# Attention: softmax sums and totals moved by DMAs on Pool's queue, with reciprocals four steps later and LayerNorm's scaling on Pool

## The chip, the cores and the metric

One core of one Trainium2 chip runs the whole program. The metric is the device time of one execution in microseconds, median of several runs. Engines are named as in the profile: PE (TensorE), with its weight loads as PEld, DVE (VectorE), ACT (ScalarE), POOL (GpSimd) and SP (SyncE, which here only issues DMAs).

## The reference

Input x is 8 batches of 1024 tokens of width 256. The program computes a feed-forward stage with routing, attention, and the feed-forward stage again, each on a LayerNorm of its input and added to it:

```
x = x + 0.5 * ffn(layernorm(x))
x = x + attention(layernorm(x))
x = x + 0.5 * ffn(layernorm(x))

attention:  xd = (x @ W_down).reshape(b, t, 16 heads, 16)
            keys, queries = xd through 16x16 maps per head, each * 16 ** -0.25; values likewise, unscaled
            out = softmax(queries @ keys^T, over keys) @ values        # per batch and head
            return out.reshape(b, t, 256) @ W_unify + b_unify
```

All of it is float32 in and out. Only attention is changed.

## The kernel before

`attention` works through 8 batches; a batch through 4 units g of four heads; a unit through 16 steps t. Steps 0 to 7 hold the first 512 queries (half 0), steps 8 to 15 the others (half 1), and within a half each step takes one block of 128 keys. In step t TensorE does three things:

- `for_exp` (L1360): four score tiles (128 keys x 512 queries, one a head) of step t + 1, into the three banks `pd`. ScalarE's exponentials (L1457) read them and free the banks.
- `for_max` (L1349): scores of step t + 13 with queries on the partitions, in two parts, for VectorE's row maxima (L1521). The maxima travel through a DRAM tensor into extra rows of the query operand, so that the exponential needs no subtraction.
- `times_v` (L1369): four heads' values times the exponentials of step t, summed in one bank `po` over the eight steps of a half. The value operand `va` has 32 columns a head: 16 values, one column of ones, 15 of zeros. So row 16 of a head's 32 rows in `po` holds the softmax totals.

Besides, a step may hold one side tile, placed by the table `side_at` (L1139): xT (transpose of the LayerNorm), xd (W_down), qk, v, all for the next batch, and for the output f, aT and u. A side tile takes a bank of the same ring of three, between the second and the third score tile.

The way of the sums is this. After steps 7 and 15 VectorE copies `po` to `os` (`values_out`, L1547). In the second step of the following half (t = 9, or t = 1 of the next unit) tile f transposes `os` on TensorE (L1378), VectorE takes the reciprocal of the totals (L1578) and multiplies (L1581) into `ao`. Once four units have passed, two tiles aT a half transpose `ao` back (L1378), ScalarE copies them to `aT` (L1478), and two tiles u multiply with W_unify (L1408); VectorE adds x and the bias and SyncE stores. aT and u of half 0 stand in steps 10, 11, 13, 14 of unit 3, those of half 1 in steps 2, 3, 5, 6 of the next batch's unit 0.

LayerNorm of the next batch runs in unit 0: VectorE's statistics in steps 0, 1, 4, 5 (L147 to L160), Pool's power -1/2 in steps 1 and 5 (L165), VectorE's scaling in steps 2, 3, 6, 7 (L173). Pool also splits the keys in two parts (`key_parts`, L1663, L1665) and adds the bias to the residual (L1690, step 8 of unit 2).

Each engine runs one instruction stream, written out by the class `Walk`, which calls each engine's `step` in the same order; nothing is reordered at run time, and a wait holds up everything behind it on its engine. Semaphores order the engines. SyncE's queue carries the loads of heads, maxima, rows and the stores.

Of the kernel before, what the change touches and what calls it, by code (L numbers as in the profile page):

```python
# [21 lines left out]
P = 128  # L22
D = 256
# [1044 lines left out]
def attention(nc, k, w, x_in, x_out, NBAT):  # L1068
# [10 lines left out]

    mscr = nc.dram_tensor("at_mscr", (4, 2, MROWS, 2, NT, P // MB, MB), F32).ap()  # L1080

    x_t, o_t = split_token_tiles(x_in), split_token_tiles(x_out)
    with ExitStack() as ctx:
# [17 lines left out]
        rec = sb("rec", [P, 4, GH], F32)  # L1101
        ao = sb("ao", [P, NT, D], F32)
        aT = sb("aT", [P, DT, NQ], F32)
# [6 lines left out]
        diagonals = Diagonals(ctx, nc, w, k, pb[0], ao[:, :, :])  # L1110

        S = lambda n: Sem(ctx, nc, "at_" + n)
        s_one = ctx.enter_context(nc.semaphore("at_s_one"))
# [6 lines left out]
        s_ld = [[S(f"s_ld{g}{p}") for p in range(2)] for g in range(4)]  # L1120
        s_mr = [S(f"s_mr{g}") for g in range(4)]
# [6 lines left out]
        s_rc = S("s_rc")  # L1128
        s_xl = S("s_xl")
# [7 lines left out]
        OUT = lambda f: [("aT", f, 0), ("aT", f, 1), ("u", f, 0), ("u", f, 1)]  # L1137
# [21 lines left out]
        splits = lambda task: task[0] == "qk"  # L1159
        half = lambda b, g, qh: 2 * unit(b, g) + qh  # L1160
        unit = lambda b, g: 4 * b + g
        next_unit = lambda b, g: (b, g + 1) if g < 3 else (b + 1, 0)

        half_ahead = lambda b, g, t: (b, g, 1) if t < NT else (*next_unit(b, g), 0)
# [10 lines left out]
        class Walk:  # L1175
# [3 lines left out]
            def __init__(self, eng, do):  # L1179
# [15 lines left out]
                do.end([self.place(task, NBAT - 1, 1, 3) for task in [("f", 1)] + OUT(1)])  # L1195
# [8 lines left out]
            def phase(self, do, b, par, g, prev=True, last=False):  # L1204
                for t in range(ST):
# [13 lines left out]
                    elif task == ("f", 1):  # L1219
                        a = self.place(task, *((b, par, g - 1) if g > 0 else (b - 1, 1 - par, 3)))  # L1220
                    elif task and task[0] in ("aT", "u") and g == 0:
# [6 lines left out]

        block = ctx.enter_context(nc.Block())

        @block.sync
        def _(eng):
            for s in (*s_xr, *(x for two in s_ld for x in two), *s_mr, s_ms, s_xl, *s_st):
                s.open(eng)
# [7 lines left out]
            def load_head(ring, b, g, j, parts_in):  # L1242
# [9 lines left out]
                for s, part in enumerate(Q_SLOTS):  # L1252
                    r1 = HALF * e + HS * s
                    src = parts[r0:r0 + HS, 0, part, c, :].rearrange("r (a q) -> r a q", a=2)
                    eng.dma_start(qa[g][r1:r1 + HS, :, p, :].bitcast(F32), src.bitcast(F32)).then_inc(s_ld[g][p].sem, 16)
                for s, part in enumerate(K_SLOTS):
                    r1 = HALF * e + HS * s
                    eng.dma_start(ka[g][r1:r1 + HS, p, :].bitcast(F32),
                                  parts[r0:r0 + HS, 1, part, c, :].bitcast(F32)).then_inc(s_ld[g][p].sem, 16)
# [9 lines left out]
            def load_maxima(b, g, qh):  # L1269
# [7 lines left out]
                for e in range(2):  # L1277
# [3 lines left out]
                    eng.dma_start(to.bitcast(F32), src).then_inc(s_mr[g].sem, 16)  # L1281
# [7 lines left out]
            class Do:  # L1289
# [38 lines left out]
                def end(self, sides):  # L1328
                    for a in sides[3:]:
# [7 lines left out]
        def _(eng):  # L1337
# [3 lines left out]
            def for_max(b, g, t, kh):  # L1341

                qh, p, qt = t // NT, t % NT // 4, t % 4
                if t in (0, NT // 2) and kh == 0:
                    eng.wait_ge(s_ld[g][p].sem, s_ld[g][p].at(16 * ULOADS * (b + 1)))
# [7 lines left out]
            def for_exp(ring, b, g, t, j, n):  # L1353

                qh, kt, e, p = t // NT, t % NT, j % 2, j // 2
                if kt == 0 and j == 0:
                    eng.wait_ge(s_mr[g].sem, s_mr[g].at(16 * MLOADS * (2 * b + qh + 1)))
# [15 lines left out]
            def side_product(ring, a):  # L1373
# [23 lines left out]
                elif a.kind == "f":  # L1397
                    eng.wait_ge(s_o.sem, s_o.at(2 * unit(a.b, a.g) + a.at[0] + 1))
                    mm = turn(lambda j: os_[:, j * P:(j + 1) * P])
                elif a.kind == "aT":  # L1400
                    f, c = a.at
                    mm = turn(lambda j: ao[:, 4 * f + j, c * P:(c + 1) * P])
                else:
                    f, h = a.at
                    for i in range(2):
                        q = (2 * h + i) * P
                        for c in range(DT):
                            mm = eng.matmul(bank[:, i * D:(i + 1) * D], aT[:, c, q:q + P], w.wu[:, c, :],  # L1408
# [3 lines left out]
            class Do:  # L1412
                def before(self, sides):
# [5 lines left out]
                    eng.wait_ge(s_one, 2)  # L1419
# [31 lines left out]
        def _(eng):  # L1451
            for s in (s_hi, *s_free):
# [5 lines left out]

            def side_out(ring, a):
                if a.kind in ("f", "u"):  # L1460
# [3 lines left out]
                if a.kind == "qk":  # L1464
                    c, f = a.at
                    if f == 0:
                        for two in s_ld[2 * c:2 * c + 2]:
                            for s in two:
                                eng.wait_ge(s.sem, s.at(16 * ULOADS * a.b))
# [7 lines left out]
                elif a.kind == "aT":  # L1477
                    ins = eng.activation(aT[:, a.at[1], :], bank[:, :], ACT.Copy)  # L1478
# [6 lines left out]
            class Do:  # L1485
                def before(self, sides):
                    for a in sides:
                        if a.kind == "v":
                            eng.wait_ge(s_one, 2)
# [9 lines left out]
                def step(self, b, par, g, t, coming, tiles, done, a, side, ahead, last):  # L1499
# [4 lines left out]
                    for j in range(2, GH if tiles else 2):  # L1504
                        exponentials(self.ring, t + 1, j, tiles[j])

# [7 lines left out]
        def _(eng):  # L1514
            norm.open_vector(eng)
            for s in (s_xn, s_mx, s_nm, s_o, s_rc):
# [32 lines left out]
            ALL, FIRST, SECOND = range(4), (0, 1), (2, 3)  # L1549

# [185 lines left out]
```

## Time and profile before

| | |
|---|---|
| median of 3 runs | 2889.71 us (2889.34 to 2901.28) |
| the profiled execution | 2896.95 us, span 2895.2 us |
| attention, in the span | about 640 to 2262 us |
| busy in the span | PE 93%, DVE 74%, ACT 63%, POOL 21% |
| granted TensorE clock, mean | 0.964 of full speed |

The busy shares are of the whole span and mix three stages. Matmuls are pipelined, so that a PE shown busy is not necessarily at its peak; idle time of an engine that nobody waits for costs nothing. A row's line number is that of the helper that issues the instruction.

### The profile page before, as it was taken

To read this page: it belongs to the slowest core of one execution; us is meant where nothing else is said; L and a number is where in the kernel's file an instruction comes from. 1 tells how busy PE (TensorE), PEld (TensorE's weight loads), DVE (VectorE), ACT (ScalarE), POOL (GpSimd) and SP (SyncE) were. 2 spreads that over 40 slices of the span, in tenths; PEclk is the share of its full clock that TensorE was granted. 3 is DMA by queue.
4 is the path that set the end of the run, shared out by engine and by line. 5 is a ranking of instruction groups with operands and counts; after the bars stand their busy time and mean duration, and the time that the engine had idled before them with its cause. 6 is when DMAs were issued, how large, how long until landed. Compare 5 with 4: busy or idle time off the path is not lost. (4 is left out here: it accounts for less than half of the span.)

```text
span 2895.2 us, 48611 instructions
## 1 busy us (share of the span) xinstructions
PE 2705.7 (93%) x17009; PEld 1644.3 (57%) x17009; DVE 2145.9 (74%) x3552; ACT 1821.3 (63%) x3409; POOL 599.8 (21%) x562
## 2 busy tenths in 40 slices
PE   5899999867999999999999999999999589999997
PEld 3799999863334334333343343433433368999886
DVE  6555456747899898998998988989895665554574
ACT  5344556632777776777777767777777444444564
POOL 3355114521100100101001001010000235521353
PEclk9899999986999999999999999999999789999998
DMA  5211113414123132131231321312310512111341
GB/s 172 66 44 44 58 45 106 133 60 75 30 50 75 33 61 54 39 62 36 50 75 33 60 55 39 62 37 50 60 28 5 173 30 80 44 44 45 102 133 63
DMA packets 164529, 181.69 MB, mean 63 GB/s; under 512 B 38472, under 2 KB 133904, under 8 KB 164368
## 3 DMA queue, kind: packets, MB, share of 16 engines
q1 hardware_dynamic: 156176, 169.03, 24.0%
q0 software_dynamic: 8192, 10.57, 1.2%
q8 instruction: 94, 1.54, 0.2%
q14 instruction: 67, 0.55, 0.1%
HBM read 97.51 MB, written 31.54 MB: 45 GB/s over the span
## 5 line engine op out<-in xcount | busy, mean ns | idle before, releaser
L1457 ACT ACTIVATE at_ex<-at_pd 128x512 f32<-128x512 f32 x2048 | 1084.7, 600 | 383.7 <-PE at_pd L1360 379.2
L1521 DVE TENSOR_REDUCE at_mxc<-at_pb 128x2 f32<-128x1024 f32 x1024 | 1219.0, 1219 | 120.8 <-PE at_pb L1349 113.8
L768 DVE TENSOR_TENSOR f_ml_hl<-f_ml_h,f_ml_hh 128x512 fp32r<-128x512 f32 (+1 forms) x384 | 287.8, 751 | 422.7 <-ACT f_ml_hh L844 421.5
L1360 PE MATMUL at_pd<-at_qa,at_ka 50*128 50x512 f32 x2048 | 583.6, 469 | 3.9 <-ACT at_ex L1457 3.2
L1360 PEld LDWEIGHTS at_pd<-at_qa,at_ka 50*128 50x128 f32 x2048 | 266.6, 185 | 538.4 <-issue 349.2
L1369 PE MATMUL at_po<-at_ex,at_va 128*32 128x512 f32 x4096 | 548.8, 608 | 0.2 <-ACT at_ex L1457 0.2
L841 ACT ACTIVATE f_ml_h<-f_ml_pL,b1T 128x512 f32<-128x512 f32 (+1 forms) x384 | 243.8, 635 | 457.9 <-PE f_ml_pL L895 446.3
L1349 PE MATMUL at_pb<-at_ka,at_qa 48*128 48x512 f32 x2048 | 433.1, 450 | 24.7 <-DVE at_mxc L1521 16.5
L910 PE MATMUL f_ml_pA<-f_wh,f_ml_hh 128*128 128x256 f32 (+1 forms) x1408 | 410.4, 291 | 3.7 <-DVE f_ml_hl L768 3.7
L912 PE MATMUL f_ml_pA<-f_wl,f_ml_hh 128*128 128x256 f32 (+1 forms) x1408 | 402.5, 286 | 0.0
L913 PE MATMUL f_ml_pA<-f_wh,f_ml_hl 128*128 128x256 f32 (+1 forms) x1408 | 402.5, 286 | 0.0
L1349 PEld LDWEIGHTS at_pb<-at_ka,at_qa 48*128 48x128 f32 x2048 | 196.0, 188 | 191.0 <-DVE at_mxc L1521 129.0
L893 PE MATMUL f_ml_pL<-f_ml_xTh,f_wh 128*128 128x512 f32 (+1 forms) x768 | 286.5, 373 | 2.8 <-DVE f_ml_xTl L763 2.8
L894 PE MATMUL f_ml_pL<-f_ml_xTl,f_wh 128*128 128x512 f32 (+1 forms) x768 | 286.2, 373 | 0.0
L895 PE MATMUL f_ml_pL<-f_ml_xTh,f_wl 128*128 128x512 f32 (+1 forms) x768 | 283.0, 368 | 0.0
L910 PEld LDWEIGHTS f_ml_pA<-f_wh,f_ml_hh 128*128 128x128 f32 (+1 forms) x1408 | 265.9, 189 | 15.9 <-DVE f_ml_hl L768 5.2
L912 PEld LDWEIGHTS f_ml_pA<-f_wl,f_ml_hh 128*128 128x128 f32 (+1 forms) x1408 | 266.0, 189 | 7.1
L913 PEld LDWEIGHTS f_ml_pA<-f_wh,f_ml_hl 128*128 128x128 f32 (+1 forms) x1408 | 265.7, 189 | 0.0
L844 ACT ACTIVATE f_ml_hh<-f_ml_h 128x512 fp32r<-128x512 f32 (+1 forms) x384 | 222.2, 579 | 20.0
L165 POOL TENSOR_TENSOR f_ml_ln_rstd<-f_ml_ln_ve,neghalf 128x4 f32<-128x4 f32 (+1 forms) x48 | 52.8, 1101 | 562.5 <-DVE f_ml_ln_ve L160 562.5
L165 POOL TENSOR_TENSOR at_ln_rstd<-at_ln_ve,neghalf 128x4 f32<-128x4 f32 x16 | 16.2, 1014 | 714.8 <-DVE at_ln_ve L160 714.8
L895 PEld LDWEIGHTS f_ml_pL<-f_ml_xTh,f_wl 128*128 128x128 f32 x768 | 148.0, 193 | 22.5
(128 smaller groups left out, 2636.6 us busy)
## 6 DMA issues: line engine op xcount, KB each, us to landing
f_wraw<-in_L_ffn_w SPq DMA_DIRECT2D x128, 256.0 KB, 2.8
at_qa<-at_parts SPq DMA_DIRECT2D x384, 64.0 KB, 2.4
at_ka<-at_parts SPq DMA_DIRECT2D x384, 64.0 KB, 2.4
f_ro_xr<-in_L_attn_x SPq DMA_DIRECT2D x16, 512.0 KB, 3.9
f_ml_xr<-in_L_attn_x SPq DMA_DIRECT2D x16, 512.0 KB, 4.2
x<-f_ml_yo SPq DMA_DIRECT2D x16, 512.0 KB, 4.0
at_xr<-x SPq DMA_DIRECT2D x16, 512.0 KB, 5.1
at_xres<-x SPq DMA_DIRECT2D x8, 1024.0 KB
```

The lines of the kernel that those rows point to most:

```text
L768: eng.tensor_tensor(hl[h % RING][:, 0:w], h32[h % 2][:, 0:w], hh[h % RING][:, 0:w].bitcast(F32), ALU.subtract).then_inc(s_lo.sem, 1)
L893: eng.matmul(out, W1(wh[wb], c, h), xTh[b][:, c, 0:w], start=(c == 0), stop=False)
L894: eng.matmul(out, W1(wh[wb], c, h), xTl[b][:, c, 0:w], start=False, stop=False)
L895: mm = eng.matmul(out, W1(wl[wb], c, h), xTh[b][:, c, 0:w], start=False, stop=(c == DT - 1))
L910: eng.matmul(out, hi, W2(wh[wb], h), start=(h == 0 and j % 2 == 0), stop=False, skip_group_check=True)
L912: eng.matmul(out, hi, W2(wl[wb], h), start=False, stop=False, skip_group_check=True)
L913: mm = eng.matmul(out, lo, W2(wh[wb], h), start=False, stop=(h == HT - 1), skip_group_check=True)
L1349: mm = eng.matmul(pb[kh][:, e * NQ:(e + 1) * NQ], qa[g][rows, qh, p, qt * P:(qt + 1) * P], ka[g][rows, p, kh * NQ:(kh + 1) * NQ], start=Tr ...
L1360: eng.matmul(pd[n % RING][:, :], ka[g][rows, p, kt * P:(kt + 1) * P], qa[g][rows, qh, p, :], start=True, stop=True).then_inc(s_full.sem, 1)
L1369: mm = eng.matmul(po[VW * j:VW * (j + 1), :], va[par][:, kt, GH * g + j, :], ex[t % 2][:, j, :], start=(kt == 0), stop=(kt == NT - 1), ski ...
L1457: eng.activation(ex[t % 2][:, j, :], pd[n % RING][:, :], ACT.Exp).then_inc(s_free[n % RING].sem, 1)
L1521: eng.tensor_reduce(mxc[:, t // NT, kh, t % NT::NT], pb[kh][:, :].rearrange("p (e k) -> p e k", e=2), AX.X, ALU.max, negate=True).then_inc ...
```

## The change

- The tiles f and aT are gone, with the tensors `ao` and `rec`. The side table places u of both halves in unit 0 of the next batch (steps 2, 4, 10, 11), and the tiles xT, xd are moved by some steps.
- ScalarE copies `po` to `os`, at the end of steps 7 and 15, behind that step's exponentials.
- Pool issues five DMAs a half. They write the sums to DRAM (`sums_out`, one step after the copy's), read the totals into `tot` (128 x 16) and the values into `aT` (`sums_in`), write the reciprocals (`totals_out`) and read them, each row 16 times, into `den` (`totals_in`). Each stage waits for the landing of the one before. `divide` multiplies `aT` with `den` on Pool once two units' heads fill 128 partitions.
- VectorE takes the reciprocals of `tot` in steps 4 and 12.
- Pool takes the power and the scaling of LayerNorm (`normalize`, steps 5 and 12 of unit 0). VectorE's statistics are in steps 2, 4, 10, 11.
- The columns 16 to 31 of a head in `va` are all ones. The load semaphores of heads are merged, so that a unit other than 0 waits for all its heads at once. Pool's bias is in step 14.

```diff
-            table = {1: ("f", 1), 9: ("f", 0)}
-            if g == 0 and not prev:
-                del table[1]
+            table = {}
             if g == 0 and prev:
-                table.update(zip((2, 3, 5, 6), OUT(1)))
-            if g == 3:
-                table.update(zip((10, 11, 13, 14), OUT(0)))
+                table.update(zip((2, 4, 10, 11), OUT(0) + OUT(1)))
+            if g == 3 and last:
+                table.update(zip((14, 15), OUT(0)))
             if g == 0 and not last:
-                table.update(zip((7, 8, 10, 11, 13, 14), XT + XD))
+                table.update(zip((7, 8, 12, 13, 14), [*XT[:2], XD[0], *XT[2:]]))
             if g == 1 and not last:
-                table.update(zip((2, 3, 5, 6, 7, 8), XD[-2:] + QK))
+                table.update(zip((1, 2, 3, 5, 6, 7, 8), XD[1:] + QK))
...
+            def values_out(b, g, t):
+                eng.wait_ge(s_pv.sem, s_pv.at(ST * unit(b, g) + t + 1))
+                if half(b, g, t // NT):
+                    eng.wait_ge(s_os.sem, s_os.at(16 * half(b, g, t // NT)))
+                eng.activation(os_[:, :], po[:, :], ACT.Copy).then_inc(s_o.sem, 1)
...
-            def values_out(b, g, t):
-                eng.wait_ge(s_pv.sem, s_pv.at(ST * unit(b, g) + t + 1))
-                eng.tensor_copy(os_[:, :], po[:, :]).then_inc(s_o.sem, 1)
+            def reciprocals(b, g, qh):
+                eng.wait_ge(s_td.sem, s_td.at(16 * (half(b, g, qh) + 1)))
+                eng.reciprocal(tot[:, :], tot[:, :]).then_inc(s_rc.sem, 1)
...
+            def normalize(ring, b, f, read):
+
+                norm.pow_step(eng, 2 * b + f, 4)
+                if read is not None:
+                    eng.wait_ge(s_full.sem, s_full.at(ring.full(read)))
+                at = slice(4 * f, 4 * f + 4)
+                norm.apply_step(eng, 2 * b + f, xn[:, at, :], xr[:, at, :], [P] * 4).then_inc(s_xn.sem, 1)
+
+            def sums_out(b, g, qh):
+                eng.wait_ge(s_o.sem, s_o.at(half(b, g, qh) + 1))
+                eng.dma_start(oscr[g, qh, :, :, :].rearrange("j r q -> (j r) q"), os_[:, :]).then_inc(s_os.sem, 16)
+
+            def sums_in(ring, b, g, qh, read):
+                eng.wait_ge(s_os.sem, s_os.at(16 * (half(b, g, qh) + 1)))
+                eng.dma_start(tot[:, :], oscr[g, qh, :, HS, :].rearrange("j (x y) -> j x y", y=HS)).then_inc(s_td.sem, 16)
+                if b > 0:
+                    eng.wait_ge(s_full.sem, s_full.at(ring.full(read)))
+                r0 = HS * GH * (g % 2)
+                eng.dma_start(aT[r0:r0 + HS * GH, qh, g // 2, :], oscr[g, qh, :, 0:HS, :]).then_inc(s_nd.sem, 16)
+
+            def totals_out(b, g, qh):
+                eng.wait_ge(s_rc.sem, s_rc.at(2 + half(b, g, qh) + 1))
+                eng.dma_start(rscr[g, qh, :, :].rearrange("j (x y) -> (j x) y", y=HS), tot[:, :]).then_inc(s_rs.sem, 16)
+
+            def totals_in(b, g, qh):
+                eng.wait_ge(s_rs.sem, s_rs.at(16 * (half(b, g, qh) + 1)))
+                if b > 0 or g > 1:
+                    eng.wait_ge(s_dv.sem, s_dv.at(4 * b + 2 * (g // 2) + qh - 1))
+                r0 = HS * GH * (g % 2)
+                src = rscr[g, qh, :, :].unsqueeze(1).broadcast_to([GH, HS, NQ])
+                eng.dma_start(den[r0:r0 + HS * GH, qh, :], src).then_inc(s_nd.sem, 16)
+
+            def divide(b, g, qh):
+                eng.wait_ge(s_nd.sem, s_nd.at(16 * 2 * (half(b, g, qh) + 1)))
+                if g % 2:
+                    eng.tensor_tensor(aT[:, qh, g // 2, :], aT[:, qh, g // 2, :], den[:, qh, :],
+                                      ALU.mult).then_inc(s_dv.sem, 1)
...
+                    past = (b, g, 0) if t >= NT else (*before(b, g), 1) if b or g else None
+                    if past and t % NT == 0:
+                        sums_out(*past)
+                    if past and t % NT == 1:
+                        sums_in(self.ring, *past, self.read[past[2]])
+                    if past and t % NT == 5:
+                        totals_out(*past)
+                    if past and t % NT == 6:
+                        totals_in(*past)
+                    if g == 0 and not last and t in (5, 12):
+                        normalize(self.ring, b + 1, t // 8, side)
+                    if past and t % NT == 7:
+                        divide(*past)
```

TensorE's tile u waits for `divide` of its half (`s_dv`). At the end Pool runs the five transfers and `divide` once more for the last half.

## Rows read from the trace of the kernel before

**Rows 1.** Windows, amid attention: PE, PEld, DVE, ACT, POOL busy us, clock, DMA share, GB/s.
```profile
1000.00:1100.00 100.00, 100.00 (x624) 40.11 (x620) 91.27 (x104) 76.29 (x151) 5.00 (x4) 1.00 0.34 66
```

**Rows 2.** Timeline: plain step 0 of batch 1; start us, length us, engine, line, operation.
```profile
899.96 1.06 PE L1369 MATMUL at_po<-at_ex,at_va 128*32 128x512 f32 x8
900.96 0.50 PE L1360 MATMUL at_pd<-at_qa,at_ka 50*128 50x512 f32 x2
901.40 0.68 DVE L1547 COPY at_os<-at_po 128x512 f32<-128x512 f32 x1
901.49 2.06 ACT L1457 ACTIVATE at_ex<-at_pd 128x512 f32<-128x512 f32 x4 [0.54 <-PE at_pd L1360]
902.14 0.18 PEld L1360 LDWEIGHTS at_pd<-at_qa,at_ka 50*128 50x128 f32 x1 [0.30 <-ACT at_ex L1457]
902.57 1.06 PE L1369 MATMUL at_po<-at_ex,at_va 128*32 128x512 f32 x8
```

**Rows 3.** Timeline: batch 1, group 0, from step 1 to xT's tile of step 7.
```profile
905.66 1.07 PE L1369 MATMUL at_po<-at_ex,at_va 128*32 128x512 f32 x8
...
912.14 1.06 PE L1369 MATMUL at_po<-at_ex,at_va 128*32 128x512 f32 x8
...
915.55 1.07 PE L1369 MATMUL at_po<-at_ex,at_va 128*32 128x512 f32 x8
...
919.80 1.06 PE L1369 MATMUL at_po<-at_ex,at_va 128*32 128x512 f32 x8
...
922.45 0.17 DVE L160 TENSOR_SCALAR at_ln_ve<-at_ln_mv 128x4 f32<-128x4 f32 x1
...
924.04 1.06 PE L1369 MATMUL at_po<-at_ex,at_va 128*32 128x512 f32 x8
...
925.70 0.66 PE L1378 MATMUL at_pd<-ident,at_xn 128*128 128x128 f32 x4
```

**Rows 4.** Timeline: batch 1, group 3, from step 9 to step 10.
```profile
1074.11 1.06 PE L1369 MATMUL at_po<-at_ex,at_va 128*32 128x512 f32 x8
...
1077.20 1.06 PE L1369 MATMUL at_po<-at_ex,at_va 128*32 128x512 f32 x8
```

**Rows 5.** Groups of instructions by line: count, busy us, mean ns, idle time before.
```profile
L700 POOL DMA_INDIRECT out<-f_ml_yo,f_ml_idx x24 | 24.3, 1012 | 20.2 <-DVE f_ml_yo L789 13.8 <-issue 6.4
...
L1663 POOL CAST at_parts<-at_xn 128x512 fp32r<-128x512 f32 x32 | 19.5, 609 | 271.2 <-ACT at_xn L1482 271.2
...
L1478 ACT ACTIVATE at_aT<-at_pd 128x512 f32<-128x512 f32 x32 | 19.3, 604 | 6.1 <-PE at_pd L1378 5.8
...
L165 POOL TENSOR_TENSOR at_ln_rstd<-at_ln_ve,neghalf 128x4 f32<-128x4 f32 x16 | 16.2, 1014 | 714.8 <-DVE at_ln_ve L160 714.8
```

**Rows 6.** The tile at_xres: Pool's operations on it, ns min/median/max.
```profile
L1690 POOL TENSOR_TENSOR at_xres<-at_xres,at_bu x32: 1265/1282/1308, 809.2 to 2157.1; 128x512 f32<-128x512 f32 x32
```

**Rows 7.** DMA issues: queue, count, KB each, median us from issue to landing.
```profile
at_xr<-x SPq DMA_DIRECT2D x16, 512.0 KB, 5.1
...
x<-at_yo SPq DMA_DIRECT2D x32, 256.0 KB, 2.2
...
f_ml_xr<-x,f_ml_idx POOLq DMA_INDIRECT x24, 3.5
```

**Rows 8.** Timeline: last unit, the V products of step 7.
```profile
2217.83 1.93 PE L1369 MATMUL at_po<-at_ex,at_va 128*32 128x512 f32 x8
```

**Rows 9.** Windows: last unit, the granted clock.
```profile
2220.00:2225.00 5.00, 4.74 (x17) 1.48 (x16) 0.53 (x1) 2.48 (x5) 0.00 (x0) 0.50 0.00 0
```

**Rows 10.** Timeline: attention's end and the next stage's first load.
```profile
2244.79 1.06 PE L1369 MATMUL at_po<-at_ex,at_va 128*32 128x512 f32 x8 [0.18 <-ACT at_ex L1457]
2245.92 0.69 DVE L1547 COPY at_os<-at_po 128x512 f32<-128x512 f32 x1 [2.01 <-PE at_po L1369]
...
2251.89 3.63 PE L1408 MATMUL at_pd<-at_wu,at_aT 128*128 128x256 f32 x8 [0.78 <-ACT at_aT L1478]
...
2262.06 2.03 SPq L259 DMA_DIRECT2D f_ro_xr<-x  x4
```

More of the change, by code:

```diff
@@ L1119, in attention @@
         s_kp = S("s_kp")
-        s_ld = [[S(f"s_ld{g}{p}") for p in range(2)] for g in range(4)]
-        s_mr = [S(f"s_mr{g}") for g in range(4)]
+        s_ld = [S("s_ld"), *[S(f"s_ld{g}") for g in range(4)]]
+        s_mr = [S(f"s_mr{i}") for i in range(2)]
         s_b = S("s_b")
@@ L1162, in attention @@
         next_unit = lambda b, g: (b, g + 1) if g < 3 else (b + 1, 0)
+        before = lambda b, g: (b, g - 1) if g else (b - 1, 3)
         half_ahead = lambda b, g, t: (b, g, 1) if t < NT else (*next_unit(b, g), 0)
@@ L1194, in __init__ @@
                         self.phase(do, b, b % 2, g, prev=b > 0, last=b == NBAT - 1)
-                do.end([self.place(task, NBAT - 1, 1, 3) for task in [("f", 1)] + OUT(1)])
+                do.end([self.place(task, NBAT - 1, 1, 3) for task in OUT(1)])
             def place(self, task, b, par, g):
@@ L1227, in phase, with units_landed @@
                     do.step(b, par, g, t, coming, tiles, done, a, side, ahead, last)
+        def units_landed(eng, b, c):
+            for g, p in ((0, 0), (0, 1), (1, 0)) if c == 0 else ((2, 0), (3, 0)):
+                eng.wait_ge(landed(g, p).sem, landed(g, p).at(loads(g, b)))
         block = ctx.enter_context(nc.Block())
@@ L1232, in _ @@
         def _(eng):
-            for s in (*s_xr, *(x for two in s_ld for x in two), *s_mr, s_ms, s_xl, *s_st):
+            for s in (*s_xr, *s_ld, *s_mr, s_ms, s_xl, *s_st):
                 s.open(eng)
@@ L1258, in load_head @@
                     eng.dma_start(ka[g][r1:r1 + HS, p, :].bitcast(F32),
-                                  parts[r0:r0 + HS, 1, part, c, :].bitcast(F32)).then_inc(s_ld[g][p].sem, 16)
+                                  parts[r0:r0 + HS, 1, part, c, :].bitcast(F32)).then_inc(landed(g, p).sem, 16)
             def ones():
@@ L1328, in end @@
                 def end(self, sides):
-                    for a in sides[3:]:
+                    for a in sides:
                         store_out(self.ring, a)
@@ L1451, in _ @@
         def _(eng):
-            for s in (s_hi, *s_free):
+            for s in (s_hi, s_o, *s_free):
                 s.open(eng)
@@ L1631, in step @@
                         turn(*half_ahead(b, g, t))
-                    if t % NT == NT - 1:
-                        values_out(b, g, t)
-                    if g == 0 and not last and t < 8:
-                        f, q = t // 4, t % 4
-                        if q < 2:
-                            stats(b + 1, f, (FIRST, SECOND)[q])
-                        else:
-                            apply(self.ring, b + 1, f, side, (FIRST, SECOND)[q - 2])
+                    if t == NT + 4:
+                        reciprocals(b, g, 0)
+                    if t == 4 and (b or g):
+                        reciprocals(*before(b, g), 1)
+                    if g == 0 and not last and t in STATS_AT:
+                        stats(b + 1, *STATS_AT[t])
                 def end(self, sides):
+                    reciprocals(NBAT - 1, 3, 1)
                     for a in sides:
@@ L1694, in end @@
                 def end(self, sides):
-                    pass
+                    past = (NBAT - 1, 3, 1)
+                    sums_out(*past)
+                    sums_in(self.ring, *past, self.read[1])
+                    totals_out(*past)
+                    totals_in(*past)
+                    divide(*past)
             Walk(eng, Do())
```

100 lines of the change are left out of this document (43 added, 57 removed).

## The prediction

> **What bounds the kernel now.** I read the page first: of the span's 2895 us, attention holds 640 to 2262 and the change touches nothing else, so everything below is about those 1620 us. The table of windows comes next. In a stretch in the middle of attention TensorE is busy all the time at a granted clock of 1.00 (its 2.4 GHz level), VectorE for 91% and ScalarE for 76% [rows 1]. A TensorE busy for 100% in modelled records does not yet say which engine sets the pace, so I went to the timeline of one step.
>
> There are 512 steps (8 batches x 4 head groups x 16), and each ends with one group of eight products with V on L1369. The distance between the starts of two such groups is the length of a step. A step with nothing on the side takes 2.61 us (899.96 to 902.57, [rows 2]). Inside it a loop closes: the first score product starts at 900.96, ScalarE has no work for 0.54 us until it lands, its exponential begins at 901.49, and the fourth score product (loading at 902.14, idle 0.30 on ScalarE) needs the bank which that exponential frees, because there are three banks for four tiles. Then come the products with V, then the next step. So a plain step is bound by this loop through TensorE and ScalarE. VectorE's two maxima (2.35 us together) fit beside it. Even the step in which VectorE also copies the sums (0.68 us at 901.40) is 2.61 long: that copy costs nothing today.
>
> A step with a side tile is longer. Read off the starts in [rows 3]: f 3.09 (902.57 to 905.66, the first of the two in [rows 2]), aT in group 0 3.24 (905.66 to 912.14 are two), u 4.25 (915.55 to 919.80), and xT 0.49 over plain like f. Step 4 of group 0 has no side tile and still takes 3.41 (912.14 to 915.55), because VectorE is behind with the LayerNorm. aT in group 3 takes 3.09 [rows 4]. These lengths return in every batch, except in batch 0's first steps and in the last unit.
>
> **The change part by part.** First what goes.
>
> (a) The f tiles: 64 in all, 1 after the walk and 1 in the last unit (taken below), so 62 x (3.10 - 2.61) = 30.4 us.
> (b) The aT tiles of group 3 in seven batches: 14 x 0.49 = 6.9.
> (c) The aT tiles of group 0: twelve x 0.63 and two (in the last batch, priced as in group 3) x 0.49 = 8.6.
> (d) VectorE's overlong step 4 in six batches: 6 x (3.41 - 2.61) = 4.8. In batch 0, whose group 0 has the same LayerNorm and no u steps beside it, I count two and a half such steps: 2.
> Together 52.7 us. The u, xT, xd, qk and v tiles keep their number and their price, in other steps.
>
> Then what comes.
>
> (e) ScalarE copies the sums. The 64 copies stand in front of the first exponential of the next step, inside the loop. The products with V end at 901.02 [rows 2]; where an engine waited for just this, it began 0.07 after the end (2245.85 to 2245.92, [rows 10]). So the copy can begin at 901.09. It lasts 0.60 (ScalarE's copy of the same shape, which stood among exponentials, [rows 5], L1478), exponentials follow each other 0.1 closer than they last, so the exponential begins at 901.59 to 901.69 instead of 901.49: 0.15 us lost, passed on through the fourth product. 62 x 0.15 = 9.3. Bounds: 0 (the 0.54 of idle hides it), and 0.60 each, 37 in all. VectorE's release of 0.68 is worth nothing here, as its copy cost nothing.
>
> (f) Pool's five transfers a half, 64 times. Half a unit is 8 x 2.61 = 20.9 us, or 21.05 with (e). On the path lie four round trips: sums out, totals in, reciprocals out, reciprocals in. Pool's indirect transfers take it 1.01 us to issue [rows 5], L700; from issue to landing 3.5 us is the row for a gather on Pool's queue, 2.2 for SyncE's 256 KB store of the same size as the sums, and 5.1 for a 512 KB load [rows 7]. I take 2.75 a trip, 11 for four, bounds 2.2 and 5.1. With the copy (0.67), the reciprocal (0.25), the product (1.28, [rows 6]) and handoffs (0.6) the chain is 13.8 us, under 21. The reciprocal waits in order on VectorE in step 4: its totals must be there about 13 us after the boundary and come after 0.9 + 2 x 2.75 + Pool's issues, some 7.5. In front of u, which waits for the product in group 0's steps 2 and 10, one and three steps are left. So the cost in the walk is 0, and the cover gone only above 4.6 us a trip (rival 1). Pool's other work in this span (its bias, 5.1 us, now in step 14, and the key parts, 1.9 us each, queued behind these waits) is needed many steps later.
>
> The Trainium skill ("DMA: Bandwidth & Descriptors", Anatomy of one DMA, SWDGE path) gives 2.0 us plus the bytes over 436 GB/s; by it the four trips would be about 9 us, and the tail below 2 us shorter. The nearest row of this queue, 3.5, lies above that.
>
> (g) Pool scales LayerNorm's tiles. For the second half of a batch the statistics end 7.07 us after the start of step 10's V products (from 915.55 to 922.62, [rows 3]), as step 11 is a u step like the one read. xT in step 13 begins 4.25 + 4.25 + 1.66 = 10.16 after that start (1.66 from 924.04 to 925.70). That leaves 3.09, less 1.01 for the power [rows 5], L165 and 0.2 of handoffs: 1.87 for four tiles, 0.47 each. The first half leaves 2.6 (0.65 each), as its steps 5 and 6 are plain. Pool's price for a 128x256 scaling is in no row. Its one-input CAST of 128x512 takes 0.61, its two-input operation 1.28 [rows 5, 6]; halved, 0.30 and 0.64. I take 0.5, nearest to these halves: 7 x (2.0 - 1.87) = 1 us. Bounds: 0 at 0.30, and 40 us if a tile costs the whole 1.28.
>
> (h) The reciprocals on VectorE, 0.25 or less each, fall in plain steps, where the maxima of a half (8 x 2.35 = 18.8) leave VectorE 2.1 us. Cost 0. Merging the load semaphores makes unit g >= 1 wait for all its heads before step 0; by the schedule its last head is issued ten or more steps before that. Cost 0.
>
> (i) The last unit has no maxima, and there the granted clock reads 0.50, the 1.2 GHz level, between 2220 and 2225, after TensorE's work had thinned out [rows 9]. Steps 8 to 15 took 27.0 us (2217.83 to 2244.79, [rows 8, 10]). With f and aT gone: six plain steps at 2.61 and two u steps (3.8 and 3.2) are 22.6; if the clock stays low, a step's products without maxima take 4.1 instead of 2.05, six of them 24.4, and 31.4 in all. u in step 14 comes 15.6 + 0.7 us after the boundary, the chain needs 13.8. Value 0, bounds -4.4 and +4.4.
>
> (j) The tail. From the last product's end (2245.85) to the next stage's first load (2262.06) it is 16.2 us now [rows 10]. After the change nothing hides the chain: 13.8 us, then from the first u product to the load 10.2 (2251.89 to 2262.06), and 1 more as the clock, already low for the first u, has then been without work for longer. 25 us, so +9. Bounds +6 (trips of 2.2) and +19 (of 5.1).
>
> **The sum.** -52.7 + 9.3 + 1 + 0 + 9 = -33.4 us. Made against the profiled execution's own 2896.95 (span 2895.2 and 1.7 around it) that is 2863.5; that execution lies 7.2 above the median of the timed runs, 2889.71, from which I get 2856.
>
> **The rivals.**
> 1. *Pool's round trips become the bound (slower).* Place: VectorE waits in order for the totals, and with it the maxima, hence TensorE. The cycle is four trips and 2.7 us of fixed work; it exceeds 21.05 from 4.6 us a trip, and at 4.7, with the longer tail, the 33 us are gone. At 4.9 it loses 1.25 x 62 = 78: 2934. At 5.1, 2983. [...] Against: transfers of this size land in 2.2 to 3.5. Pool's two-input operations in the busy walk last 1265 to 1308 ns [rows 6], so VectorE does not hold Pool up. Chance 0.08. The Trainium skill ("SBUF — State Buffer", SBUF: two separate sides) says that Pool can't write descriptors while VectorE runs an operation that takes their shared port. If the maxima were such, each issue could wait a further 1.2 us and a trip would reach 4.0 to 4.7, so by that rule this rival decides; the row of Pool's operations shows no such wait.
> 2. *Pool's LayerNorm is late for xT.* At 1.0 us a tile, 2.1 + 1.4 us a batch: 2856 + 24 = 2880; at 1.28, 2895. For: thin margins. Against: halves of the rows. Chance 0.12.
> 3. *The copy costs its full length.* 0.60 at 62 boundaries: 2856 + 28 = 2884. Against: 0.54 of idle, mostly after the V products' end. Chance 0.09.
> 4. *The side tiles' time is not given back*, because VectorE is the hidden bound at 91% busy and plain steps grow. Against: a plain step holds 2.61 even with VectorE's copy in it [rows 2]. Half of (a) to (c) lost: 2880. Chance 0.05.
>
> **How the numbers follow.** My forecast has 0.66; its own range is 2843 to 2870 (copy 0 to 0.3, tail +6 to +14, last unit either way). Less than 0.5%, 14 us, can't be told from no change. Faster by more: 0.66, half of rival 2, and a little of 3 and 4, 0.77. Same: 0.13. Slower: rival 1 and the end of rival 2, 0.10. For eight in ten, 2842 to 2884.
>
> **What would show it.** Plain steps still 2.61; steps 1 and 9 of every unit at 2.61; the boundary step at 2.7 to 2.8 with ScalarE's copy just ahead of an exponential; group 0's step 4 at u's 4.25; VectorE without any wait for totals; xT without a wait on Pool; 24 to 26 us from the last V product to the next stage. I am wrong if VectorE's reciprocal or TensorE's u shows waits on transfers, if Pool's scaling takes over 0.65 us, or if the boundary steps exceed 3 us.

## The result, and the profile after

The changed kernel took 2905.36 us (median of 12 runs, 2897.8 to 2917.7) against 2892.74 for the kernel before beside it (12 runs, 2888.1 to 2901.3): a ratio of 1.004, with an interval of 1.0024 to 1.0056. It is slower, by 0.4%; the forecast was 2856, with a range from 2842 to 2884. The profiled execution took 2914.12 us (span 2912.4, granted clock 0.949), against 2896.95 and 0.964 before, so the span grew by 17.2 us.

First the page of the changed kernel: busy time by engine.

```profile
PE 2688.8 (92%) x16625; PEld 1612.4 (55%) x16625; DVE 2066.9 (71%) x3366; ACT 1832.6 (63%) x3441; POOL 909.9 (31%) x970
```

Pool went from 21% to 31% of the span, VectorE from 74% to 71%, which does not yet say where the time went. Next the window amid attention (columns as in [rows 1]).

```profile
1000.00:1100.00 100.00, 99.99 (x620) 36.69 (x612) 91.03 (x97) 81.75 (x163) 24.23 (x32) 1.00 0.44 93
```

Here, mostly in groups 1 to 3 of a batch, nothing is wrong: TensorE is busy all the time at the 2.4 GHz level. So the loss is local, and the lengths of single steps have to show it. Step 0 of batch 1 and the boundary ahead of it, answering [rows 2] (changed kernel, timeline):

```profile
899.28 0.60 ACT L1468 ACTIVATE at_os<-at_po 128x512 f32<-128x512 f32 x1
...
899.78 2.06 ACT L1462 ACTIVATE at_ex<-at_pd 128x512 f32<-128x512 f32 x4
...
900.85 1.07 PE L1379 MATMUL at_po<-at_ex,at_va 128*32 128x512 f32 x8
...
903.45 1.06 PE L1379 MATMUL at_po<-at_ex,at_va 128*32 128x512 f32 x8
```

A plain step is 2.60 (900.85 to 903.45), and the exponential follows ScalarE's copy by 0.50, less than the copy lasts. The boundary step, read over all batches, is 2.70, or 0.09 over plain. The steps that held f and aT are plain now. What grew is group 0, in its steps 6, 7, 13 and 14. Here are steps 12 to 14 of batch 3:

```profile
1330.46 1.04 POOL L165 TENSOR_TENSOR at_ln_rstd<-at_ln_ve,neghalf 128x4 f32<-128x4 f32 x1 [7.29 <-DVE at_ln_ve L160]
...
1331.68 4.84 POOL L173 TENSOR_SCALAR at_xn<-at_xr,at_ln_mv,at_ln_rstd 128x256 f32<-128x256 f32 x4 [0.18 <-POOL at_ln_rstd L165]
...
1331.98 1.06 PE L1379 MATMUL at_po<-at_ex,at_va 128*32 128x512 f32 x8
...
1336.66 1.09 PE L1388 MATMUL at_pd<-ident,at_xn 128*128 128x128 f32 x4 [2.95 <-POOL at_xn L173]
...
1338.83 1.93 PE L1379 MATMUL at_po<-at_ex,at_va 128*32 128x512 f32 x8
...
1343.29 1.07 PE L1379 MATMUL at_po<-at_ex,at_va 128*32 128x512 f32 x8
```

Step 12 to 13 is 6.85 long (1331.98 to 1338.83) where 3.10 was due. Pool begins right behind VectorE's statistics and its own power; its four scalings then take 4.84 us, and xT's transposes wait 2.95 for the last. The same transposes last 1.09 instead of 0.66 [rows 3], and the V products behind them 1.93 instead of 1.06. The windows say why (around that place, columns as above):

```profile
1333.00:1337.00 4.00, 1.05 (x10) 0.64 (x7) 1.46 (x3) 1.25 (x3) 4.00 (x4) 0.81 0.61 101
1337.00:1341.00 4.00, 4.00 (x18) 1.35 (x18) 1.23 (x1) 1.68 (x3) 1.96 (x3) 0.50 0.60 97
1341.00:1345.00 4.00, 4.00 (x26) 1.89 (x25) 2.44 (x2) 2.94 (x6) 0.66 (x1) 0.84 0.13 37
```

TensorE was busy for 1.05 of 4 us while it waited, and the granted clock then stood at 0.50, its 1.2 GHz level, through the whole second window and for parts of the two around it (from about 1335.5 to 1342.3). So the pause is paid again: step 13 to 14 is 4.46 long instead of 3.10. In batches 1 and 2 the wait is the same 2.95 but the clock falls later: step 12 to 13 is 5.91 there, with transposes of 0.63. By line and in the waits of the whole execution:

```profile
L173 POOL TENSOR_SCALAR at_xn<-at_xr,at_ln_mv,at_ln_rstd 128x256 f32<-128x256 f32 x56 | 67.8, 1216 | 2.6 <-POOL at_ln_rstd L165 2.3 <-PE at_pd L1370 0.2
...
L1388 PE MATMUL at_pd<-ident,at_xn 128*128 128x128 f32 x128 | 25.8, 341 | 39.2 <-POOL at_xn L173 32.9 <-DVE at_xn L173 6.3
```

A tile costs Pool 1.216 us; two waits a batch make 32.9 us in 14. The feared waits are absent: Pool's transfers land in 2.1 to 4.1 us, and it is Pool that waits for VectorE in front of writing the reciprocals, not the other way round (changed kernel, DMA issues, columns as in [rows 7]).

```profile
at_oscr<-at_os POOLq DMA_DIRECT2D x64, 256.0 KB, 2.4
...
at_aT<-at_oscr POOLq DMA_DIRECT2D x64, 128.0 KB, 4.1
at_den<-at_rscr POOLq DMA_DIRECT2D x64, 128.0 KB, 4.1
...
at_tot<-at_oscr POOLq DMA_DIRECT2D x64, 8.0 KB, 2.1
at_rscr<-at_tot POOLq DMA_DIRECT2D x64, 8.0 KB, 2.3
```

And from the waits (us in total, times, longest):

```profile
POOL at_rscr L1687 <- DVE at_tot L1556: 416.6, 57, 11.5
...
DVE at_tot L1556 <- DMA at_tot<-at_oscr: 27.7, 2, 21.7
```

VectorE waited for totals only twice, in the last unit and behind it, when it had no maxima left to take. The tail, answering [rows 10] (changed kernel, timeline):

```profile
2254.59 1.06 PE L1379 MATMUL at_po<-at_ex,at_va 128*32 128x512 f32 x8
2255.72 0.60 ACT L1468 ACTIVATE at_os<-at_po 128x512 f32<-128x512 f32 x1 [2.86 <-PE at_po L1379]
2256.61 0.60 POOL L1673 DMA_DIRECT2D at_oscr<-at_os  x1 [19.49 <-ACT at_os L1468]
2259.24 0.69 POOL L1679 DMA_DIRECT2D at_tot<-at_oscr  x1 [2.03 <-DMA at_oscr<-at_os]
...
2261.95 0.58 POOL L1687 DMA_DIRECT2D at_rscr<-at_tot  x1 [1.41 <-DVE at_tot L1556]
2264.40 0.62 POOL L1696 DMA_DIRECT2D at_den<-at_rscr  x1 [1.86 <-DMA at_rscr<-at_tot]
2268.37 1.26 POOL L1702 TENSOR_TENSOR at_aT<-at_aT,at_den 128x512 f32<-128x512 f32 x1 [3.35 <-DMA at_den<-at_rscr]
2269.77 3.75 PE L1413 MATMUL at_pd<-at_wu,at_aT 128*128 128x256 f32 x8 [14.12 <-POOL at_aT L1702]
...
2280.02 2.04 SPq L259 DMA_DIRECT2D f_ro_xr<-x  x4
```

The next stage's first load is issued at 2280.02: 25.4 us after the start of the last V products, where it was 17.3 (2244.79 to 2262.06). **The account of +17.2 us:** the walk begins 1.8 earlier; from first to last V products it takes 1545.6 instead of 1534.1, +11.6; the tail +8.2; the last stages −0.8. Within the walk, batches 0 to 6 give +3 (194.0 a batch before from the second on, 193.7 to 195.0 after) and the last unit +8.7. All that (a) to (d) should bring, some 6.4 us a batch, has gone into steps 6, 7, 13 and 14 of group 0.

### The profile page after: what moved, and what is told of

It reads as the page before. It is cut to its first block and busy times, and to the rows that moved or that the text cites. A ratio compares the mean times of both kernels' runs of the same rounds, so it can differ in the third digit from the quotient of the medians.

```text
span 2912.4 us, 48128 instructions
## 1 busy us (share of the span) xinstructions
PE 2688.8 (92%) x16625; PEld 1612.4 (55%) x16625; DVE 2066.9 (71%) x3366; ACT 1832.6 (63%) x3441; POOL 909.9 (31%) x970
## 5 line engine op out<-in xcount | busy, mean ns | idle before, releaser
L1370 PE MATMUL at_pd<-at_qa,at_ka 50*128 50x512 f32 x2048 | 614.5, 475 | 3.7 <-ACT at_ex L1462 3.7
L1379 PE MATMUL at_po<-at_ex,at_va 128*32 128x512 f32 x4096 | 561.4, 621 | 0.0
L1359 PE MATMUL at_pb<-at_ka,at_qa 48*128 48x512 f32 x2048 | 417.0, 451 | 23.1 <-DVE at_mxc L1530 16.0
L1687 POOL DMA_DIRECT2D at_rscr<-at_tot x64 | 38.0, 594 | 416.6 <-DVE at_tot L1556 416.6
L1379 PEld LDWEIGHTS at_po<-at_ex,at_va 128*32 128x32 f32 x4096 | 81.2, 108 | 142.7 <-issue 138.8
```

What stands on the lines that cost most here:

```text
L1359: mm = eng.matmul(pb[kh][:, e * NQ:(e + 1) * NQ], qa[g][rows, qh, p, qt * P:(qt + 1) * P], ka[g][rows, p, kh * NQ:(kh + 1) * NQ], start=Tr ...
L1370: eng.matmul(pd[n % RING][:, :], ka[g][rows, p, kt * P:(kt + 1) * P], qa[g][rows, qh, p, :], start=True, stop=True).then_inc(s_full.sem, 1)
L1379: mm = eng.matmul(po[VW * j:VW * (j + 1), :], va[par][:, kt, GH * g + j, :], ex[t % 2][:, j, :], start=(kt == 0), stop=(kt == NT - 1), ski ...
```

## The experiments

My theory: the removal brings what I had worked out; Pool's scaling, at 1.2 us a tile and in steps too close to its reader, takes it back, partly by way of the granted clock. The rivals: side tiles whose time isn't given back, the round trips, ScalarE's copy, and the last unit's clock. E1, E2, E3 and E4 ran beside a before of 2892.6; E5, E6, E8 and E9 beside 2892.3; E10, on its own, beside 2888.1.

**E1: VectorE scales again**, behind its step 5 and at the start of its step 12; Pool keeps the power.

```diff
+                    if g == 0 and not last and t == 12:
+                        apply(1, self.ring, b + 1, side)
...
+                    if g == 0 and not last and t == 5:
+                        apply(0, self.ring, b + 1, side)
...
-                norm.apply_step(eng, 2 * b + f, xn[:, at, :], xr[:, at, :], [P] * 4).then_inc(s_xn.sem, 1)
```

> The changed kernel with LayerNorm's scaling back on VectorE (first half behind step 5, second half at the start of step 12); Pool takes the power only, everything else as changed. Theory A (Pool's scaling, 1.22 us a tile and 4.84 for four, arrives after xT wants it, 7 us a batch in group 0's steps 6, 7, 13 and 14): these steps come back to 2.6 and 3.1 to 3.6, 40 to 47 us less than the changed kernel, so about 2860. Rival B (VectorE's statistics in steps 10 and 11 are themselves too late, whoever scales): step 13 stays at 5 us or more, about 2890. Rival C (the DMAs on Pool's queue slow the loads or Pool): no step changes, about 2905.

2874.6 us, ratio 0.9946 (0.9927 to 0.9965), batches of 189.6 to 191.1. So most of the time went into Pool's scaling. The median is 31 us under the changed kernel's and not the 40 to 47 that I expected: VectorE, busy for 93% to 97% of these stretches, is late too (step 7 3.6 to 3.7, step 13 4.2, where Pool also stretched its scaling, as the last section shows). In batches 4 and 5 step 14 is 4.47 instead of 3.09, behind a wait of only 0.76 (timeline of E1, batch 4, and the window behind it):

```profile
1507.26 0.63 PE L1388 MATMUL at_pd<-ident,at_xn 128*128 128x128 f32 x4 [0.76 <-DVE at_xn L173]
...
1508.96 1.87 PE L1379 MATMUL at_po<-at_ex,at_va 128*32 128x512 f32 x8
```

```profile
1509.20:1512.40 3.20, 3.20 (x15) 0.99 (x8) 1.79 (x3) 1.76 (x4) 0.76 (x2) 0.50 0.61 100
```

**E2: Pool scales, but earlier,** and so do VectorE's statistics in front of it.

```diff
-            STATS_AT = {2: (0, FIRST), 4: (0, SECOND), 10: (1, FIRST), 11: (1, SECOND)}
+            STATS_AT = {0: (0, FIRST), 1: (0, SECOND), 5: (1, FIRST), 6: (1, SECOND)}
...
-                    if g == 0 and not last and t in (5, 12):
+                    if g == 0 and not last and t in (2, 8):
```

> The changed kernel with Pool still scaling, but earlier: VectorE's statistics in steps 0, 1, 5, 6 and Pool's power and scaling in steps 2 and 8 of group 0; xT stays in steps 7, 8, 13, 14. Theory A (Pool is late by the schedule, not because it is used): no wait of xT on Pool, steps 7, 13, 14 at 3.10, 45 to 49 us less than the changed kernel, about 2858. Rival B (VectorE is the bound in group 0, statistics anywhere cost): some 10 to 20 us less only. Rival C (Pool's scaling slows VectorE or the DMAs by sharing something): steps of group 0 stay long wherever it stands, 2890 to 2905.

2862.1 us, ratio 0.9892 (0.9874 to 0.9909). A tile still takes Pool 1.217 us, but nobody waits for it (timeline of E2, batch 1: Pool's work from step 8 on, and xT of step 13):

```profile
914.69 1.05 POOL L165 TENSOR_TENSOR at_ln_rstd<-at_ln_ve,neghalf 128x4 f32<-128x4 f32 x1
...
915.92 4.84 POOL L173 TENSOR_SCALAR at_xn<-at_xr,at_ln_mv,at_ln_rstd 128x256 f32<-128x256 f32 x4 [0.18 <-POOL at_ln_rstd L165]
...
932.25 0.66 PE L1388 MATMUL at_pd<-ident,at_xn 128*128 128x128 f32 x4
```

Batches are 187.6, steps 7, 13 and 14 are 3.10 each. That is 6.4 us a batch under before, and 7 under the changed kernel. It is the order, not Pool's use, that costs. Step 6 of group 0 tells the two parts of this edit apart: in full batches it takes 3.00 to 3.03 in the changed kernel, in E1, E9 and E10 alike, whoever scales and at whatever price, and 2.60 only with the early statistics. So its 0.4 us belongs to VectorE's statistics, and the rest goes with Pool's scaling.

**E3: the last unit kept busy.** In the last unit TensorE repeats score products in place of the missing ones for the maxima; nobody reads them.

```diff
                     if ahead:
                         for_max(*ahead, 0)
+                    else:
+                        filler(g, t, 0)
```

> The changed kernel with one addition: in the last unit, where no row maxima are left to take, TensorE repeats the score products for maxima (four a step from step 3 on) into the two banks that nobody reads any more. Output unchanged. Theory A (the last unit runs at 4.07 us a step because the granted clock falls to 0.50 when TensorE's work thins out): clock 1.00 through the last unit, steps 2.61, 12 to 14 us less than the changed kernel, about 2892. Rival D (the last unit is long because of Pool's transfers or ScalarE): steps stay at 4 us or get longer by the added products, 2905 to 2915.

2902.0 us, ratio 1.0031 (1.0020 to 1.0041). In the profile the last unit is 23.8 us from step 7 on instead of 33.1, and the clock there 1.00; the span is 14 under the changed kernel's, as expected. The median, for which I had about 2892, fell by 3 only: a miss, and no difference by the intervals. But the nine runs lie within 8.7 us, where the changed kernel's twelve lie within 20. The last unit's low clock is not met in every profile (low in the changed kernel, E2 and E9, for a part of it in the kernel before, high in E1, E4, E5 and E10). The timed runs have a mean clock of the whole span. Of the changed kernel's twelve, four have 0.947 to 0.950 and took 2910.2 to 2917.7, the profiled one among them; eight have 0.954 to 0.957 and took 2897.8 to 2906.8. E3's nine all have 0.954 to 0.959. That fits a low last unit in some four of twelve runs, which a median hardly shows; a clock record per unit they don't have, so this is argued, not shown.

**E4: the kernel before, with Pool scaling** in steps 2 and 6, and nothing else of the change. VectorE's own scaling goes, and its next statistics wait until Pool has scaled.

```diff
-                    if g == 0 and not last and t in (1, 5):
-                        norm.pow_step(eng, 2 * (b + 1) + t // 4, 4)
+                    if g == 0 and not last and t in (2, 6):
+                        normalize(self.ring, b + 1, t // 4, side)
```

> The kernel before with one part of the change alone: Pool scales LayerNorm's tiles (steps 2 and 6 of group 0, statistics where they were, xT in steps 7, 8, 10, 11 as before); all else as before. Theory A (the price of 1.22 us a tile is harmless when three steps lie between): step 4 of group 0 goes from 3.41 to 2.61, no wait on Pool, 5 to 8 us less than before, about 2886. Rival C (Pool's scaling itself is the trouble by its price or by what it shares with VectorE): xT waits on Pool, 10 to 40 us more than before.

2885.2 us, ratio 0.9973 (0.9963 to 0.9983). Step 4 of group 0 fell from 3.41 to 2.79 (I had 2.61) and the batch from 194.0 to 193.4: relieving VectorE is a gain where xT comes late enough.

**E5: the kernel before, with ScalarE's copy of the sums.**

```diff
+                eng.activation(os_[:, :], po[:, :], ACT.Copy).then_inc(s_o.sem, 1)
...
-                eng.tensor_copy(os_[:, :], po[:, :]).then_inc(s_o.sem, 1)
```

> The kernel before with one part of the change alone: ScalarE copies the sums at the end of steps 7 and 15, VectorE no longer does. Theory A (the copy sits in the loop through TensorE and ScalarE and costs what the changed kernel's rows show, 0.09 us a boundary): steps 8 and 0 go from 2.61 to 2.70, 5 to 6 us more than before, about 2898. Rival E (the copy is hidden, and VectorE's release pays): 0 to 5 us less than before. Rival F (full price, 0.5 to 0.6 a boundary): 2925.

2891.96 us, ratio 0.9999 (0.9989 to 1.0009); batches 194.3 instead of 194.0. The boundary step is 2.70, the 0.09 of the changed kernel, but part comes back in group 0, where VectorE is relieved of the copy: steps 2 and 3 fall from 3.24 to 3.10, step 4 from 3.42 to 3.35. I had expected 5 to 6 us; the effect can't be told from zero.

**E6: E2 and E3 together.**

> Early statistics and Pool's scaling in steps 2 and 8, together with the added products that keep TensorE at work in the last unit. Theory A: last unit's steps 8 to 15 from 33.5 to about 23.8 us, clock 1.00 there in every run, so up to 10 us less than the early statistics alone where its runs had the low clock, about 2854 in the median and a narrower spread. Rival D (the next stage starts at a lower clock or the tail grows by as much, given back later): 2860 to 2863.

2854.8 us, ratio 0.9875 (0.9860 to 0.9890), within 4.4 us over four runs; batches 187.6, the last unit 23.8.

**E8: E6 with a shorter tail.** For the last half alone the totals go straight into `den`, each row 16 times, and VectorE takes the reciprocals there: two trips fewer.

```diff
+                    eng.reciprocal(den[r0:r0 + HS * GH, 1, :], den[r0:r0 + HS * GH, 1, :]).then_inc(s_rc.sem, 1)
...
+                    eng.tensor_tensor(aT[:, 1, 1, :], aT[:, 1, 1, :], den[:, 1, :], ALU.mult).then_inc(s_dv.sem, 1)
...
+                    src = oscr[3, 1, :, HS:HS + 1, :].broadcast_to([GH, HS, NQ])
+                    eng.dma_start(den[r0:r0 + HS * GH, 1, :], src).then_inc(s_td.sem, 16)
```

> The kernel of early statistics and busy last unit, with the last half's way made shorter: Pool reads the totals straight into the 64 x 512 tile, each row 16 times, VectorE takes the reciprocals there and multiplies, so two of the four round trips fall away and the other two run side by side. Theory A (the tail is the serial round trips, 13.6 us from ScalarE's copy to u): that stretch becomes 8 to 10 us, 3.5 to 5 us less than the kernel without this. Rival G (the tail is set by the landing of the values, 4.1 us, and VectorE's reciprocal of 512 elements costs what the trips did): within 1 us of it.

2851.6 us, ratio 0.9862 (0.9847 to 0.9877), the lowest median, but the intervals of E6 and E8 overlap. From the end of ScalarE's copy to u it is 10.9 us instead of E6's 13.2 (I had 8 to 10): VectorE's reciprocal of 64x512 lasted 3.35 us, which eats much of the two trips. And from the last V products to the load it is 24.5 against E6's 24.9, so 2.0 of these 2.3 us are lost again behind the start of u. Its second group of products took 3.62 us here against 1.97, as the granted clock was 0.54 where it was 1.00 in E6. The timeline of E6:

```profile
2212.54 1.97 PE L1421 MATMUL at_pd<-at_wu,at_aT 128*128 128x256 f32 x8 [0.83 <-issue]
```

And of E8:

```profile
2210.67 3.62 PE L1421 MATMUL at_pd<-at_wu,at_aT 128*128 128x256 f32 x8 [0.83 <-issue]
```

**E9: two tiles instead of four.** The changed kernel, with Pool scaling only two of the four tiles of the second half; the other two are left out.

```diff
-                norm.apply_step(eng, 2 * b + f, xn[:, at, :], xr[:, at, :], [P] * 4).then_inc(s_xn.sem, 1)
+                norm.apply_step(eng, 2 * b + f, xn[:, at, :], xr[:, at, :], [P] * 4,
+                                range(2) if f else range(4)).then_inc(s_xn.sem, 1)
```

> The changed kernel, but Pool scales only two of the four tiles of each batch's second half (the other two keep old contents, so this part of the computation is left out), 2.43 us less of Pool's work before xT of step 13. Theory A (the wait for Pool is one for one, and the pause of TensorE costs a second time because the granted clock drops after it): step 13 goes from 5.9 to 6.9 to about 3.7, step 14 from 4.46 to 3.10 with no low-clock transposes, together 3.6 to 4.6 us a batch, 25 to 32 us less than the changed kernel, about 2877. Rival H (no clock share, the time follows Pool alone): 2.4 us a batch, 17 us, 2888. Rival B (VectorE's statistics hold it up): no gain.

2889.3 us, ratio 0.9996 (0.9984 to 1.0008). Pool does 2.43 us less a batch, and a full batch falls by 3.4 to 5.1. The surplus is the clock: xT in step 13 waits 0.56 instead of 2.95, its transposes take 0.63 instead of 1.09, and step 14 is 3.10 instead of 4.46; in batches 3 to 6 step 8 takes back 1.3. The two spans are 25.4 us apart, as theory A had it (25 to 32), but the medians only 16, which is rival H's number. The profiled execution here, close to its median, has the low clock in the last unit (34.0 us from step 7 on), and the changed kernel's median run may not have it, as said under E3. So it is the steps that speak for the clock's share, not the median.

**E10: one arithmetic operation instead of two.** Pool subtracts the mean and leaves the multiplication out.

```diff
+                    last = eng.tensor_scalar(xn[:, j, :], xr[:, j, :], norm.mv[:, j - 4 * f, 0:1], None, ALU.subtract)
```

> The changed kernel in its own steps, but Pool's scaling does only the subtraction of the mean: one arithmetic operation and one per-partition operand instead of two (the multiplication by the inverse deviation is left out). It asks what Pool's 1.216 us for a 128x256 tile is made of, and whether my sum holds in the changed kernel's own order once the tile is cheap. Theory A: Pool pays for each of the two arithmetic operations, about 0.6 us each; then a tile takes 0.6, four take 2.4 against the 1.87 that the order leaves in front of xT in step 13, 0.6 us late, and against 2.6 in front of step 7, not late. The batches fall from 194.6 to about 188.5, the walk by about 43 us, the profiled span from 2912 to about 2869, the median from 2905 to 2855 to 2868 by the last unit's clock. That would be my forecast of 2856 with the term (g) at 0.6 a tile. Theory B: the price hangs on the elements read with a per-partition operand, whatever the number of operations: the tile stays at 1.2 us, batches stay at 194.6 and the median at 2905. Between the two (0.9 a tile): four take 3.6, 1.8 late in step 13 and 1.0 in step 7, about 191.5 a batch, 2885.

2875.7 us, ratio 0.9963 (0.9945 to 0.9980), between the two theories, where I had 2885 and 191.5 a batch; the before beside it is also some 4 us lower than the others'. By line (E10):

```profile
L1670 POOL TENSOR_SCALAR at_xn<-at_xr,at_ln_mv 128x256 f32<-128x256 f32 x56 | 51.0, 921 | 2.5 <-POOL at_ln_rstd L165 2.3 <-PE at_pd L1370 0.2
```

So 0.30 us belongs to the second operation with its operand, and a single one still takes 0.92 for half the columns of a CAST of 0.61 [rows 5]. Batches are 191.2: 3.4 less for 2.4 of Pool's time. In front of step 13's xT TensorE pauses for 1.75 (E10, timeline; the window behind it):

```profile
1324.09 0.63 PE L1388 MATMUL at_pd<-ident,at_xn 128*128 128x128 f32 x4 [1.75 <-POOL at_xn L1670]
1325.37 1.93 PE L1379 MATMUL at_po<-at_ex,at_va 128*32 128x512 f32 x8
```

```profile
1325.00:1328.00 3.00, 3.00 (x16) 0.70 (x12) 1.23 (x1) 1.44 (x3) 1.48 (x2) 0.53 0.62 101
```

Even this pause is followed by the 1.2 GHz level, and step 14 is 4.3 to 4.4. A pause of 1.60, in front of step 7's xT, was followed by a step 8 of 3.18 in batches 1 to 6 of the changed kernel; in E9 by 3.19 in batches 1 and 2 and by 4.4 in 3 to 6. So the length of a pause alone does not decide, and what does stays open.

## Why the prediction was wrong, step by step

- **(a) to (d)** held. With steps 1 and 9 of every unit plain and group 0's step 4 gone, I had 7.0 us for a full batch, 6.2 with the measured (e) taken off; E2, where Pool is out of the way, saves 6.4. Rival 4 falls.
- **(e)** 0.15 forecast, 0.09 measured: 5.6 us instead of 9.3 over 62 boundaries, and E5, which has nothing else, shows no loss. Rival 3 falls.
- **(f)** held: no wait for a trip in the walk; the two waits for totals are at the end. Landing takes 2.1 to 4.1, where I had bounds of 2.2 and 5.1, and rival 1 falls. Nor did Pool's issues wait behind VectorE: their means are 0.59 to 0.69. The Trainium skill ("DMA: Bandwidth & Descriptors", Anatomy of one DMA, SWDGE path) gives 2.0 us plus the bytes over 436 GB/s. An estimate by it agrees for the sums (2.6 against 2.4 measured) and the totals (2.0 against 2.1 and 2.3), not for the 128 KB into 64 partitions (2.3 against 4.1).
- **(g) is the step that failed.** I took 0.5 us for a 128x256 scaling, halving Pool's CAST and its two-input operation over 128x512; it is 1.216. The four take 4.84 where 1.87 and 2.6 us were left. By that alone this is (3.0 + 2.2) x 7 = 36 us, and the trace has 32.9 us of waits. The seven batches of the changed kernel less those of E2 are 50.8, since the pauses also bring the low clock (E9, E10), for which the sum had no term: some 10 us in step 14 and 4 in step 13. Some 3 are VectorE's statistics in step 6. I had 1 for all of it. The mechanism was my rival 2; at its end of 1.28 I had priced 2895, with no term for the clock after a pause, and gave it 0.12. The sign that I had written down ("if Pool's scaling takes over 0.65 us") is the one that came.
- Rows of before would have warned me: the same operation on VectorE in the same shape (by line), Pool's two-input operation over 256 columns instead of 512 (by line), and VectorE's over 512 (the tile at_yo; ns min/median/max).

```profile
L173 DVE TENSOR_SCALAR at_xn<-at_xr,at_ln_mv,at_ln_rstd 128x256 f32<-128x256 f32 x64 | 22.9, 403 | 1.4 <-POOL at_ln_rstd L165 1.4
...
L677 POOL TENSOR_TENSOR f_ml_xs<-f_ml_xr,f_b2s 64x256 f32<-64x256 f32 x16 | 15.1, 943 | 0.0
...
L1589 DVE TENSOR_TENSOR at_yo<-at_pd,at_xres x32: 674/690/693, 892.5 to 2258.4; 128x512 f32<-128x512 f32 x32
```

  Where both engines did a two-input operation over 128x512, Pool took 1.28 and VectorE 0.69, 1.9 times. On 0.40 that gives 0.75, already over the 0.65 that the order allowed; the real factor is 3.0. And halving was not safe: half the columns, in half the partitions too, took Pool 0.94 and not 0.64. That is near rival 2's price of 1.0, for which I had 2880.
- **(h)** held: the reciprocals last 0.25, and in groups 2 and 3 every step is plain but the boundaries and the four with v tiles (3.09).
- **(i)** 0 forecast with bounds of 4.4 either way: in the changed kernel's profile the clock stayed low from about 2213, steps took 4.07, and the last unit was 33.1 from step 7 where before had 27.0: +6.1, and +2.6 in its steps ahead of that, where I had priced nothing. Its window, to be held against [rows 9]:

```profile
2213.00:2218.00 5.00, 4.74 (x17) 1.19 (x20) 0.00 (x0) 3.03 (x7) 0.00 (x0) 0.50 0.00 2
```

  At the high clock it is 22.4 to 23.8. So both ends occur, and the upper bound was 1.7 us too narrow, or 4.3 with the steps ahead.
- **(j)** +9 forecast, +8.2 measured. From the end of the last products (2255.65) to u it is 14.1 us against 13.8, from u to the load 10.3 against 11.2.

Span against span the forecast was -33.4 and the result +17.2, 50.6 apart. Of these (g), with the clock and step 6, makes 49.8, (i) 8.7, (e) -3.7, (j) -0.8 and the stages outside attention -2.6, which leaves under 1.

Without (g), and with (i) at the high clock, the change is a gain: E6 gives 2854.8 where I had 2856. That this is so close is partly luck. E6 has another order, and its span is 45.7 under before where the sum had 33.4: (e) cost 3.7 less, the last unit gave 3.2 back, the tail was 1.4 shorter, the stages outside attention 2.0, (g)'s own 1 fell away, and about 1 is left over. The medians lie 37.6 apart, since the profiled execution before lay above its median and E6's below.

## What to carry to other kernels

Before work moves to another engine, find its very form (operation, number of per-partition operands, shape) in a row of that engine, and don't halve a row for half the columns. If there is none, take its row on the old engine times the widest known ratio: here that gives 0.75, which is over the slack and calls for a run of this one operation first, though it still is short of the 1.216. Compare the price with the slack in front of the reader, and move the producer earlier when they meet: the changed kernel was 13 us slower than before with Pool's work close to its reader, and 30 us faster with it some steps sooner. And a wait in front of a busy TensorE is priced with the low clock behind it: here some 1.3 us more in the next step for a pause of 1.75 to 2.95, and sometimes after 0.76 to 1.60.

## What the runs showed of the hardware

- Pool's TENSOR_SCALAR over 128x256: 1.216 us with two operations and two per-partition operands (VectorE: 0.403), 0.92 with one of each; its CAST over 128x512 0.61, its two-input operation 1.28, and over 64x256 0.94.
- After a pause of 1.75 us (E10) TensorE's granted clock read 0.53 over the next 3 us, around one of 2.95 (changed kernel) 0.50 over 4, and V products took 1.93 instead of 1.06. This came in every full batch. After 1.60 it came in some batches, after 0.76 in two of six (E1), after 0.56 in none (E9).
- VectorE's scaling stretched beside Pool's two-input operation. The Trainium skill ("SBUF — State Buffer", SBUF: two separate sides) has the two engines share a port; E1's timeline agrees: four tiles took 1.43 us with no Pool arithmetic beside them, and 2.71 with Pool's CAST and two-input operation beside them, where the last tile alone took 1.44.

```profile
912.91 1.43 DVE L173 TENSOR_SCALAR at_xn<-at_xr,at_ln_mv,at_ln_rstd 128x256 f32<-128x256 f32 x4
...
935.49 2.71 DVE L173 TENSOR_SCALAR at_xn<-at_xr,at_ln_mv,at_ln_rstd 128x256 f32<-128x256 f32 x4
...
935.97 0.72 POOL L1664 CAST at_parts<-at_xn 128x512 fp32r<-128x512 f32 x1 [0.59 <-ACT at_xn L1489]
...
936.77 1.28 POOL L1666 TENSOR_TENSOR at_parts<-at_xn,at_parts 128x512 fp32r<-128x512 f32 x1
```

- Pool issues a direct transfer in 0.59 to 0.69 us, against 1.00 to 1.17 for an indirect one (kernel before).
